# Adding a subject's projection to x: a tile of batches n and n + 64 in place of batches 2n and 2n + 1

## The reference

```python
w = weights[subjects]                      # (128, 128, 128), from (8, 128, 128)
out = jnp.einsum('bct,bcd->bdt', x, w)
return x + out                             # (128, 128, 1024)
```

## Time and profile before

| | before |
|---|---|
| median of 3 runs | 325.02 us (324.95 to 325.21) |
| the profiled execution's own time | 324.97 us |
| its span (first to last instruction) | 323.2 us |
| PE, DVE, ACT busy, share of the span | 72%, 61%, 41% |
| bytes moved, mean rate | 134.81 MB, 417 GB/s |

### The profile page before, as it was taken

The page is one execution under the profiler, slowest core; times in us unless marked ns, Lnnn a source line. Parts: engine busy times, 40 slices in busy tenths (PEclk is TensorE's granted clock), DMA queues, the critical chain, the costliest instruction groups (busy, mean ns, idle before and its releaser), DMA issues.

```text
span 323.2 us, 3792 instructions
## 1 busy us (share of the span) xinstructions
PE 234.3 (72%) x1024; PEld 104.4 (32%) x1024; DVE 196.0 (61%) x261; ACT 132.3 (41%) x131; POOL 0.8 (0%) x7
## 2 busy tenths in 40 slices
PE   0199999999878778777687686786776867867400
PEld 0044444444333324333333233242333332423200
DVE  3238888888855756656657557566575575663500
ACT  4026646556543433434424434334244343343400
POOL 1000000000000000000000000000000000000000
PEclk9999999999999999999999999999999999999955
DMA  7999999999999999999999999999999999999994
GB/s 288 426 421 401 422 427 431 422 426 430 425 427 429 426 426 429 427 426 428 427 427 427 427 429 427 425 432 425 427 429 426 427 429 426 426 429 427 423 430 208
DMA packets 18967, 134.81 MB, mean 417 GB/s; under 512 B 2065, under 2 KB 2578, under 8 KB 2578
## 3 DMA queue, kind: packets, MB, share of 16 engines
q1 hardware_dynamic: 9744, 67.64, 50.0%
q10 hardware_dynamic: 9218, 67.11, 49.2%
HBM read 67.63 MB, written 67.11 MB: 417 GB/s over the span
## 4 chain that ended last, share of the span: by engine, by line
DMA 64%; PE 22%; DVEq 3%; DVE 3%; issue 2%; ACT 0%; ACTq 0%; SPq 0%
DMA out<-x_ring 47%; PE product L189 22%; DMA x_ring<-x 16%; DVEq L114 2%; DMA weight_halves<-weights 1%; DVE x_ring L123 1%; DVE weight_ring L115 1%; DVE x_ring L122 0%; DVEq L40 0%; ACT weight_bank L151 0%; DVEq L115 0%; DVE weight_bank L108 0%; ACTq L163 0%; SPq L77 0%; ACTq L162 0%
## 5 line engine op out<-in xcount | busy, mean ns | idle before, releaser
L189 PE MATMUL product<-x_ring,weight_ring 64*128 64x512 f32 x1024 | 234.3, 602 | 69.1 <-DMA x_ring<-x 54.2
L189 PEld LDWEIGHTS product<-x_ring,weight_ring 64*128 64x128 f32 x1024 | 104.4, 189 | 198.1 <-issue 192.2
L122 DVE TENSOR_TENSOR x_ring<-product,x_ring 64x1024 f32<-64x1024 f32 x64 | 77.9, 1216 | 96.9 <-PE product L189 96.9
L159 ACT COPY x_ring<-product 64x1024 f32<-64x1024 f32 x64 | 64.5, 1008 | 168.8 <-PE product L189 168.8
L123 DVE TENSOR_TENSOR x_ring<-product,x_ring 64x1024 f32<-64x1024 f32 x64 | 78.5, 1227 | 0.8
L160 ACT COPY x_ring<-product 64x1024 f32<-64x1024 f32 x64 | 64.2, 1004 | 0.8
L115 DVE COPY weight_ring<-weight_bank 64x256 f32 x128 | 36.9, 288 | 7.0 <-issue 4.3
L102 DVE COPY weight_bank<-weight_halves 64x1024 f32<-64x1024 f32 x2 | 1.4, 688 | 4.7 <-DMA weight_halves<-weights 4.6
L151 ACT COPY weight_bank<-weight_halves 64x1024 f32<-64x1024 f32 x2 | 2.2, 1115 | 2.1 <-DMA weight_halves<-weights 2.1
L151 ACT ACT_TABLE_LOAD x1 | 1.3, 1283 | 1.4 <-PEq L206 1.4
L108 DVE TENSOR_TENSOR weight_bank<-weight_bank,eye 64x512 f32<-64x512 f32 x2 | 1.4, 686 | 0.3 <-ACT weight_bank L151 0.2
## 6 DMA issues: line engine op xcount, KB each, us to landing
x_ring<-x SPq DMA_DIRECT2D x64, 1024.0 KB, 12.9
out<-x_ring ACTq DMA_DIRECT2D x64, 1024.0 KB, 39.4
weight_halves<-weights SPq DMA_DIRECT2D x1, 512.0 KB, 4.0
subject_row<-subjects ACTq DMA_DIRECT2D x1, 0.5 KB
```

Source lines behind the costliest of these rows:

```text
L122: dve.tensor_tensor(x_ring[LOW, slot, 0, :], low[LOW, :], x_ring[LOW, slot, 0, :], add)
L159: act.copy(x_ring[LOW, slot, 1, :], low[HIGH, :])
L189: last = pe.matmul(product[slot % PRODUCTS][a][:, cols], weight_ring[half, slot, r, :], x_ring[half, slot, r, cols], start=r == 0, stop=r ...
```

## The change

A tile holds batches n and n + 64. The two patterns in DRAM are written with the pair's number in front, (a n) for (n a), and the address of the subject's number follows: the second batch's is 64 places after the first's in place of one.

```diff
-    x_of_tile = x.rearrange("(n a) (h r) t -> n (a h) (r t)", a=2, r=R)
-    out_of_tile = out.rearrange("(n a) (h r) t -> n (a h) (r t)", a=2, r=R)
+    x_of_tile = x.rearrange("(a n) (h r) t -> n a h (r t)", a=2, r=R)
+    out_of_tile = out.rearrange("(a n) (h r) t -> n a h (r t)", a=2, r=R)
...
-                    subject = dve.value_load(subject_row[0:1, bass.ds(tile * 2 + a, 1)], min_val=0, max_val=S - 1)
+                    subject = dve.value_load(subject_row[0:1, bass.ds(tile + a * TILES, 1)], min_val=0, max_val=S - 1)
```

## The result

| | before | after |
|---|---|---|
| median | 324.99 us (324.90 to 325.21, 4 runs) | 2,514.22 us (2,514.06 to 2,514.33, 4 runs) |
| ratio | | 7.7209, 95% interval 7.7023 to 7.7395 |
| the profiled execution's span | 323.2 us | 2,512.4 us |
| mean rate | 417 GB/s | 54 GB/s |

Where the runs of a kernel further down spread by more than 1.5%, a ratio to before rests on the fastest of them, and the range of all of them stands beside it.

What follows compares the result with a forecast made beforehand. The prediction took the kernel to be bound by its DMA transfer rate: 16,384 packets / 2 engines x 0.307 us = 2,515 us, plus 10.6 us outside the full rate, gave 2,525 us, range 2,486 to 2,688.

Steps and rivals of the forecast that it cites:

- The number of engines: Loads and stores: a DRAM pattern with outermost count 2 sends each transfer through two DMA engines; given 88%.
- The rate of an engine: DMA engines: each moves 26.7 GB/s, 0.307 us per 8 KB packet, whether alone or one of sixteen.
- The six slices at 27 GB/s: End of the earlier run, stores alone: six 0.3 us slices with one engine left, no faster than one of sixteen.
- The fixed part: Weights' load, start, uneven end and 1.8 us outside the span: 10.6 us outside the full rate, kept whole.
- What was hidden: Per tile, matmuls of 3.70 us (7.4 at half clock), additions of 2.5 and copies of 2.0 hide under 39.3 us of transfers.
- An issue: Issuing a transfer on ACT or SP: 0.34 to 0.73 us each, hidden in the cover of 39 us per tile.
- The cover at the end: Last tile's matmuls and sums lie beside stores still queued; without that cover, some 10 us more at the end.
- A: Rival on loads and stores: the pattern is dealt out by rows, all 16 engines stay, about 325 us; 6%.
- B: Rival on loads and stores: only one direction, say the loads, is narrowed to two engines, 1,425 us; 4%.
- C: Rival on engine rate: two engines, each at most twice as fast, since sixteen shared a limit of 427 GB/s; 1,268 us; 2%.

## Why the prediction was right, point by point

- **The number of engines.** "Split along the outermost count" gave two; 8,322 and 8,848 packets are the numbers it named. Its rows had only the counts 1 and 128, so there the two was inferred; the result shows it, and counts of 4 and 8 follow the same rule with rates of 107 and 212 GB/s.
- **The rate of an engine.** The six slices at 27 GB/s said that an engine alone is no faster, and two engines made 53.6. From 100 to 2,400 us the DMA view of the changed kernel has:

```profile
DMA packets 15271, 123.18 MB, mean 54 GB/s; under 512 B 236, under 2 KB 236, under 8 KB 236
```

  123.18 MB / 2,300 us / 2 = 26.78 GB/s, or 0.3059 us for 8 KB. I had 0.307 from the 427 GB/s of sixteen engines, 26.7 each: 8,192 x 0.0011 = 9 us too much.
- **The fixed part.** 2,514.2 - 8,192 x 0.3059 = 8.3 us against the 10.6 taken over; both are remainders of a sum, and no row has them by themselves. With the 9 us above that is the whole of the miss, 2,525 for 2,514.2, 0.4%.
- **What was hidden.** A tile's matmuls took 5.1 to 6.7 us, under the 7.4 allowed for half the clock. They begin at half the clock, and it rises during the tile: for the tile that starts at 1,225.32 us the granted clock is 0.50 (1.2 GHz) up to 1,228 us and 0.89 from there to its end. So PE came to 15% of the span, between the tenth and the double of it that the prediction gave, and 380.2 us lies between the 234.3 of before and their double.
- **An issue.** I priced it at 0.34 to 0.73 us. On ACT it took 0.53, on SP 38.4. The conclusion held, the price not: SP's issue lasts as long as a tile's transfers, as if it waited for room behind earlier loads (inferred; no row shows that room), and no load comes late by it.
- **The cover at the end.** The prediction named stores as the longer queue, from landing times of 39.4 and 12.9 us. That had turned: SP had handed over its last load by 2,362.0 us, and its tile was multiplied at 2,478.6, some 117 us later and the time of three tiles; of stores, less than one tile was left by then (9.3 us up to the last issue and at most 5 after it). The timeline of the end:

```profile
2478.59 6.71 PE L189 MATMUL product<-x_ring,weight_ring 64*128 64x512 f32 x16 [33.35 <-DMA x_ring<-x]
...
2487.88 0.52 ACTq L163 DMA_DIRECT2D out<-x_ring  x1
```

  From the issue to the end of the span 24.5 us are left, and the last store needs 64 x 0.306 = 19.6 of them for itself. At most 5 us of other stores were still queued, so the 9 us of the last tile's arithmetic were only just covered, which is luck as far as the prediction goes. Had it not been, the end would have been some microseconds later, within the range.
- **The rivals.** A (16 engines, 325 us) failed at the step that two runs 32 MB apart might be dealt out by rows; 128 partitions and 1 MB in a transfer, which both kernels have, did not keep the rate, 54 GB/s against 427. B (1,425 us) did not come about, but its price was near: the two kernels with one narrow direction measured 1,435 and 1,464. C (1,268 us) failed as the earlier trace rows said: 53.6 GB/s, not over 60.

## What to carry to other kernels

Before merging or splitting a dimension of a DRAM pattern, look at the outermost count that it leaves: 128 became 2 here, and with it 16 engines became 2, though bytes, rows and data packets stayed the same and the SBUF side kept its 128 partitions. On SP's and ACT's queues the small packets per transfer show it in the profile. Where the layout asks for two runs, put the longer count outside (64 x 2 cost nothing, 2 x 64 a factor of 7.7), if the rest of the kernel can take partitions that alternate between the two; this one's matmuls can't as they stand. Cutting the transfer in two halves is a mend with a price of its own: 64 rows into partitions 0 to 63 move at half the rate of 128 rows or of partitions 32 to 95.

## What was not expected

- A transfer can keep all 16 engines busy, by a DMA share of 0.99 to 1.02, and move 207 GB/s in place of 424. A full DMA line does not say that the rate is full; the GB/s line does.
- Stores show this limit as sharply as loads: 207 from partitions 0 to 63, 419 from 32 to 95.
- 16 engines by count are not one rate: 64 x 2 rows ran at 325.19 us, 16 x 8 at 390.25 (372.86 at the least), with the same packets. For the 16 x 8 the cause stays open.
